# Attention: two-step value blocks, four maxima banks, and a denominator summed by GpSimd, DMA and one direct tile

## The reference, cut to what matters

```python
q, k, v = jnp.moveaxis(qkv, 2, 0)
scale = HD ** (-0.5)
attn = jnp.einsum('blhd,bmhd->bhlm', q, k) * scale
attn = jax.nn.softmax(attn, axis=-1)
out = jnp.einsum('bhlm,bmhd->blhd', attn, v).reshape(B, L, D)
```

## Time and profile before

| | before |
|---|---|
| median of 3 runs | 3703.89 us |
| lowest, highest | 3703.32, 3704.92 us |
| profiled execution, span | 3696.8 us |
| TensorE, weight loads, VectorE, ScalarE, GpSimd busy | 3452.4, 2197.3, 2266.1, 1552.4, 1775.8 us |
| attention's value blocks, first to last start | 994.5 to 2784.6 us |

### The profile page before, as it was taken

How to read it: one execution, slowest core, us unless ns; L and a number is a source line. 1 busy time by engine, 2 the same in 40 slices (tenths; PEclk the granted TensorE clock), 3 DMA queues, 4 the chain that set the end, 5 groups by cost and what they waited for, 6 DMA issues and landing times. The chain is left out here.

```text
span 3696.8 us, 51173 instructions
## 1 busy us (share of the span) xinstructions
PE 3452.4 (93%) x17516; PEld 2197.3 (59%) x17516; DVE 2266.1 (61%) x3547; ACT 1552.4 (42%) x2751; POOL 1775.8 (48%) x527
## 2 busy tenths in 40 slices
PE   7899996997999999999999999999995779999999
PEld 6488885775544444444444444444434658888887
DVE  1378874444978788788788887887715932222222
ACT  0111114341166666666656666666662242222222
POOL 1033321001288788787887887877885500000000
PEclk9999998997699999999999999999997889999999
DMA  4122224446201222102222022200004641111100
GB/s 163 66 93 88 91 80 172 172 158 183 46 17 34 43 47 44 38 16 44 47 48 44 7 44 47 47 10 13 7 6 154 216 146 68 40 40 40 37 32 23
DMA packets 158137, 250.59 MB, mean 68 GB/s; under 512 B 46939, under 2 KB 68699, under 8 KB 151774
## 3 DMA queue, kind: packets, MB, share of 16 engines
q1 hardware_dynamic: 147166, 230.96, 21.1%
q10 hardware_dynamic: 10752, 16.79, 1.5%
HBM read 158.89 MB, written 88.08 MB: 67 GB/s over the span
## 5 line engine op out<-in xcount | busy, mean ns | idle before, releaser
L1147 DVE TENSOR_REDUCE att_mx<-att_pM 128x1 f32<-128x512 f32 x2048 | 1267.9, 680 | 336.2 <-PE att_pM L1213 334.0
L1104 ACT ACTIVATE att_prob<-att_pS 128x512 f32<-128x512 f32 x2048 | 1080.4, 601 | 772.8 <-PE att_pS L1261 765.2
L1083 POOL TENSOR_TENSOR att_acc<-att_acc,att_prob 128x2048 f32<-128x2048 f32 x288 | 1327.5, 4609 | 129.2 <-ACT att_prob L1104 104.1
L1213 PE MATMUL att_pM<-att_ks,att_qs 96*128 96x512 f32 x2048 | 855.1, 432 | 54.7 <-DVE att_mx L1147 33.6
L1261 PE MATMUL att_pS<-att_qs,att_ks 98*128 98x512 f32 x2048 | 868.8, 430 | 10.2 <-ACT att_prob L1104 8.0
L1261 PEld LDWEIGHTS att_pS<-att_qs,att_ks 98*128 98x128 f32 x2048 | 386.2, 190 | 555.1 <-ACT att_prob L1104 385.7
L1228 PE MATMUL att_pO<-att_prob,att_V 128*32 128x512 f32 x4096 | 548.7, 608 | 0.7 <-ACT att_prob L1104 0.7
L1213 PEld LDWEIGHTS att_pM<-att_ks,att_qs 96*128 96x128 f32 x2048 | 405.4, 198 | 200.5 <-DVE att_mx L1147 120.3
L1627 DVE TENSOR_TENSOR mlp_us<-mlp_tu,mlp_us 128x512 fp32r<-128x512 f32 x128 | 89.7, 700 | 536.0 <-ACT mlp_us L1600 536.0
L1670 PE MATMUL mlp_pu<-mlp_hs,mlp_W 128*128 128x512 f32 x1536 | 370.7, 391 | 18.9 <-DVE mlp_W L1619 18.9
L1689 PE MATMUL mlp_pa<-mlp_W,mlp_us 128*128 128x512 f32 x1536 | 368.8, 389 | 0.0
(11 more groups left out here) (181 smaller groups left out, 2984.7 us busy)
## 6 DMA issues: line engine op xcount, KB each, us to landing
qk_d<-qkv_qs SPq DMA_DIRECT2D x64, 512.0 KB, 2.7
att_qs<-qk_d SPq DMA_DIRECT2D x48, 512.0 KB, 7.4
att_ks<-qk_d SPq DMA_DIRECT2D x48, 512.0 KB, 13.8
gat_xT<-in_xT SPq DMA_DIRECT2D x32, 256.0 KB, 3.1
gat_xrow<-in_x SPq DMA_DIRECT2D x32, 256.0 KB, 2.8
x_d<-gat_x SPq DMA_DIRECT2D x32, 256.0 KB, 2.1
qkv_xr<-x_d SPq DMA_DIRECT2D x8, 1024.0 KB, 5.8
v_d<-qkv_vs SPq DMA_DIRECT2D x32, 256.0 KB, 2.0
```

The costliest lines, as they stand in the source:

```text
L1083: nc.gpsimd.tensor_tensor(acc[half][:], old[:], new[:], ALU.add).then_inc(added, 1)
L1104: nc.scalar.activation(prob[step % PR][:, c, :], pS[n % 3][:], ACT.Exp, scale=SCALE).then_inc(exp_done, 1)
L1147: nc.vector.tensor_reduce(mx[:, n // 4, n % 4:n % 4 + 1], bank(g, n)[:], AX.X, ALU.max).then_inc(m_read, 1)
L1213: nc.tensor.matmul(bank(g, n)[:], qs[k][0:KD, h, t * P:(t + 1) * P], ks[k][0:KD, h, mc * 512:(mc + 1) * 512], start=True, stop=True).then_ ...
```

## The change

- **Values** are made for two steps at a time: at even steps, after the third score, TensorE runs the value blocks of the two steps before.
- **Maxima banks**: `pM` has four banks, filled in one sequence (`place`); `pZ` is gone.
- **Denominator**: of the 16 tiles of a half, nine are added by GpSimd in eight additions (tiles 0, 1, 3, 5, 7, 9, 11, 13, 14). Six (`SENT`: 2, 4, 6, 8, 10, 12) are gathered in a tile `gathered` by DMA: SP copies the first, GpSimd issues the other five as accumulating DMAs, each behind the landing of the one before. Tile 15 goes directly. At step 4 of the next half TensorE multiplies these three by ones in a score bank, which takes a turn between the scores (`turns_of`).
- **Reciprocal**: ScalarE copies the sums; SP copies one of each 32 equal rows, as 128x16, into `packed`; VectorE inverts that; SP writes it to DRAM (`z_d`) and spreads it back over `rec`. GpSimd makes the product with `oc`, between its additions.
- `prob` has eight buffers, `qs` and `ks` three. Stores of the result move from ScalarE's queue to SP's. The groups are written out, without the loop.

The diff, cut to its core:

```diff
-        U = 4
-        PR = 4
-        ADDED = [0, 1, 2, 4, 5, 6, 8, 9, 11, 12, 13]
-        FINISH = 2
-        INVERT = 4
+        U = 3
+        PR = 8
+        SENT = [2, 4, 6, 8, 10, 12]
+        LAST = MT - 1
+        ADDED = [t for t in range(LAST) if t not in SENT]
+        FINISH = 4
+        INVERT = 6
+        SCALED = 5
-        pM = [m.ps(f"pM{i}") for i in range(3)]
-        pO, pZ = m.ps("pO"), m.ps("pZ")
+        pM = [m.ps(f"pM{i}") for i in range(4)]
+        pO = m.ps("pO")
...
+            def send_first(n):
+                step = n % 2 * MT + SENT[0]
+                sp.wait_ge(exp_done, exps(n // 2, step))
+                if n >= 1:
+                    sp.wait_ge(exp_done, turns_of[n - 1] + 1)
+                sp.dma_start(gathered[:], prob[step % PR][:]).then_inc(first_sent, 16)
+            def reciprocals(n):
+                sp.wait_ge(exp_done, turns_of[n] + 1)
+                for c in range(4):
+                    row = rec[c * HD:c * HD + 1, :].rearrange("a (i x) -> a i x", x=16)
+                    sp.dma_start(packed[c * HD:(c + 1) * HD, :], row).then_inc(z_packed, 16)
+                sp.wait_ge(inverted, n + 1)
+                sp.dma_start(io["z_d"][n % 2].rearrange("c (i x) -> (c i) x", x=16), packed[:]).then_inc(z_kept, 16)
+                sp.wait_ge(z_kept, 16 * (n + 1))
+                for c in range(4):
+                    sp.dma_start(rec[c * HD:(c + 1) * HD, :], io["z_d"][n % 2, c:c + 1, :].to_broadcast([HD, 512])).then_inc(z_spread, 16)
...
+            def send(n, j):
+                step = n % 2 * MT + SENT[j]
+                pool.wait_ge(exp_done, exps(n // 2, step))
+                if j == 1:
+                    pool.wait_ge(first_sent, (n + 1) * 16)
+                else:
+                    pool.wait_ge(sent, (n * (len(SENT) - 1) + j - 1) * 16)
+                nc.gpsimd.dma_start(gathered[:], prob[step % PR][:], accum_op=ALU.add).then_inc(sent, 16)
...
+                        if ADDED[i] - 1 in SENT[1:]:
+                            send(n, SENT.index(ADDED[i] - 1))
+                        if i == SCALED and n >= 1:
+                            pool.wait_ge(added, n * NA + i)
+                            scale(n - 1)
...
+                elif t == SENT[0]:
+                    act.wait_ge(first_sent, (at // MT + 1) * 16)
+                elif t in SENT:
+                    act.wait_ge(sent, (at // MT * (len(SENT) - 1) + SENT.index(t)) * 16)
...
+            def invert(n):
+                dve.wait_ge(z_packed, 64 * (n + 1))
+                nc.vector.reciprocal(packed[:], packed[:]).then_inc(inverted, 1)
...
+                        if c == 2 and step % 2 == 0 and (g or step):
+                            behind(*divmod(g * ST + step - 2, ST))
+                            behind(*divmod(g * ST + step - 1, ST))
+                            if step % MT == FINISH and (g or step >= MT):
+                                finish(2 * g + step // MT - 1)
```

More of the change, by code:

```diff
@@ L1269, in body @@
+            for q in range(NM):
+                maxima(0, q)
+            for q in range(EARLY):
+                maxima(1, q)
+            top_of(0)
+            for q in range(EARLY, LEAD * 4):
+                maxima(1, q)
+            pe.wait_ge(cleared, 1 + U)
+            for g in range(NG):
+                pe.wait_ge(top_rows[g % U], (g // U + 1) * 32)
+                pe.wait_ge(v_loaded[g % 2], (g // 2 + 1) * 16)
                 for step in range(ST):
-                    if step == ST - LEAD + 1 and before(g, NG - 1):
+                    if step == ST - LEAD + 1 and g + 1 < NG:
@@ L1291, in _ @@
-            groups(pe, body)
-            behind(NG - 1, U - 1, ST - 1)
-            finish(NG, 0)
+                    for c in range(4):
+                        scores(g, step, c)
+                        if c == 2 and step % 2 == 0 and (g or step):
[3 more added lines that the diff above has]
+                                finish(2 * g + step // MT - 1)
```

402 lines of the change are left out of this document (202 added, 200 removed).

## The result

The change makes the kernel slower: 3755.61 us (median, 3751.48 to 3758.88) beside 3703.61 us for the kernel before on the same chip, a ratio of 1.0148 with a 95% interval of 1.0132 to 1.0163. The forecast was 3565 us.

The account below looks back on a forecast made before the run. TensorE was taken to bound 15 groups: 112.9 - 5.0 - 5.7 - 3.7 + 0.8 = 99.3, plus 4.5 = 103.8 us, x15 = -136.5; with the end, 3703.9 - 138.5 = 3565 us. Range 3505 to 3840, the forecast's own 3500 to 3625.

Parts of the forecast that it names:

- TensorE's sum: Attention groups: TensorE's time falls from 112.9 to 99.3 us a group, before any wait for packed sums.
- the fourth bank: Maxima in two-step blocks: four banks hold TensorE's lead of up to 1.5 us over VectorE, costed at nothing.
- The terms for the ones blocks and for VectorE: Per group: fewer ones blocks, all behind value blocks, save 5.7 us; TensorE's time lost to VectorE goes, 3.7 us.
- D: Gather chain: time from one accumulating send's issue to the next, taken as 6.6 us; up to 7.7 free.
- the formula: Gather chain: beyond D of 7.7 us, a half lasts 11.2 + 5D.
- Up to 4 us later, still in time: Fifth send sharing DMA engines with the load batch: up to 4 us later, within its 5 us margin.
- The late packed sums: Half with the loads: VectorE waits for sums packed behind the batch, +4.5 us once a group.
- The end: Last group and closing: last group saves 10 us; chain landing and three more copies for reciprocals cost 8.
- The signs: Right: groups 99 to 104 us, sends within 6.5; wrong: sends 8 apart, DMA-released exponentials, lower TensorE clock.
- Rival 1: Gather chain becomes the bound: D 8.9 us, group 121.3, time 3850 us; turns at D 8.05; chance 0.26.
- Rival 2: Chain fits outside the load batch, not in it: sends 4 us late, group 108, about 3630 us; chance 0.20.
- Rival 3: VectorE becomes the bound in eight-tile stretches: one more 2.5 us wait per half, 3640 us; chance 0.06.

Follow-up runs that it names:

- kernel 6: Changed kernel without the five accumulating sends (kernel 2), and with three maxima banks instead of four: 3583.56 us, ratio 0.969 to the kernel before.
- kernel 1: Changed kernel without the q, k and v loads of the later groups, stale data used again: 3598.64 us, ratio 0.9719 to the kernel before.
- kernel 9: Changed kernel with the five accumulating sends of each half issued as plain copies: 3514.82 us, ratio 0.9503 to the kernel before.
- kernel 2: Changed kernel without the five accumulating sends and the waits for them: 3503.46 us, ratio 0.9462 to the kernel before.
- kernel 4: Changed kernel with five gathered tiles (2, 4, 6, 8, 10) instead of six: 3691.65 us, ratio 0.9974 to the kernel before.
- kernel 11: Changed kernel with five gathered tiles spread out (2, 4, 7, 9, 12), loads as they were: 3630.52 us, ratio 0.9805 to the kernel before.
- kernel 8: Changed kernel, six gathered tiles, loads split and moved behind the last send of each half: 3629.04 us, ratio 0.9809 to the kernel before.
- kernel 10: Changed kernel with five gathered tiles spread out (2, 4, 7, 9, 12) and loads split behind last sends: 3546.95 us, ratio 0.9589 to the kernel before.
- kernel 12: Changed kernel, six gathered tiles, whole load batch waiting for the last send of the half before: 3728.47 us, ratio 1.0064 to the kernel before.
- kernel 3: Changed kernel with the group's loads issued later, behind the store of a result: 3735.96 us, ratio 1.009 to the kernel before.

## Why the prediction was wrong, point by point

**TensorE's sum was right.** With the sends away a group takes 99.8 us, forecast 99.3. The two-step blocks save the 5.0 us that I gave them (5.1), and the fourth bank covers what I said it does, at 5.0 us a group (kernel 6). The terms for the ones blocks and for VectorE (-5.7, -3.7) were tested only in the sum. Net of the waits that they bring, two-step blocks are worth only 3.1.

**The step that failed is the price D of one send and what the batch does to it.** I took D = 6.6 us on the assumption that half of the second read overlaps the first. It is 7.9 without loads in the half shown of kernel 1 and 8.1 in the mean of all its halves: 7.3 of landing, the rest issue and waiting. Kernel 9 shows the term that was too small: the addition costs 2.6 us, as much as a whole pass, and not 1.35. My sum called anything up to 7.7 free and thus gave this chain no cost; with D = 8.1 the half must be 51.8 and not 49.65 by the formula. Measured it is 52.2, which is the 4.6 us a group of kernel 1 against kernel 2. The Trainium skill (Collectives: The Full Stack, "The bandwidth ceiling: the fold count and why AG != RS != AR") says of the adding transfers of a collective that they read two sources and so run at half the rate. The time of a local addition in this trace agrees: less the 2.1 us of the earlier trace rows it is 5.2 us beside 2.6, and the D of 7.9 that I worked out from it and then did not take is nearly the measured one. For the plain copy the Trainium skill (DMA: Bandwidth & Descriptors, "Anatomy of one DMA - SWDGE (gpsimd) path") gives 2.0 us and bytes over 436 GB/s, an estimate of 4.4 us. The trace agrees: 4.4 at the least and 4.7 in the median (kernel 9).

**"Up to 4 us later, still in time"** was the second half of the same failure. I priced the send in the batch as sharing bandwidth fairly. It landed after 15.8 us in the stretch shown, after 18 us in kernel 4, up to 18.3 in kernel 11, about as long as the 17.5 us of the batch itself, though the send moves 1 MB beside its 3.5. That is +8 us and more for that send instead of 4, and the slack of 5 us was gone with D already. D also set how they meet: I had the fifth send go out 1 us ahead of the loads, and in the stretch shown it went out 7.7 us behind the first of them (1561.40 and 1569.15). It cost 10.3 us a group.

**The late packed sums** (+4.5) did not come: VectorE waited 0.8 us in 8.7 groups. In the changed kernel the sends were late first: the closing sum itself stood 7 us back, and by then the batch had passed (its last load landed at 1588.3, the packing was issued at 1591.77). But the term was too large as well. In kernels 2 and 9 no send is late and the loads stand where they stood, and yet VectorE waits for the packed sums only 15.6 and 16.6 us in ten groups. The line of kernel 2:

```profile
DVE att_packed L1236 <- DMA att_packed<-att_rec: 15.6, 11, 1.8
```

Their groups of 99.8 and 99.7 leave 0.5 us above the 99.3 for it, where I had 4.5. The mechanism as such exists: where the loads were moved behind a last send the waits are 56.2, 30.9 and 106.2 us in 1000 (kernels 8, 10 and 12).

**Together:** 99.8 + 4.6 + 10.3 = 114.7 where I had 99.3 + 0 + 4.5 = 103.8. The difference of 10.9, x15 = 163 us, is most of the 190.6 by which the forecast missed.

**The end** was the other miss: -2 forecast, +20.6 measured. From the last closing block on it is 2833.09 to 2852.01, 18.9 us, before 2789.92 to 2800.90, 11.0. These +7.9 look like my +8, but by luck: my 8 was to hold the landing of the chain as well. TensorE's timeline shows that landing, which comes on top:

```profile
2818.33 1.04 PE L1293 MATMUL att_pS<-att_prob,att_ones 128*32 128x512 f32 x8
2833.09 1.94 PE L1293 MATMUL att_pS<-att_gathered,att_ones 128*32 128x512 f32 x8 [13.72 <-DMA att_gathered<-att_prob]
```

TensorE is through with its scores and waits 13.72 us for the last of the sends, where it waited 3.89 us for GpSimd before: +9.8. With no more tiles to compute, nothing hides the chain's end. The remaining +2.9 stand ahead of these waits, where I had -10. I had taken the two halves of the last group to be bound by the chain at 44 us each. From one half's first send to the next's (2742.45 to 2794.82) it is 52.4, and in this stretch the chain is not what holds it: ScalarE's longest wait for a gather is 0.68 us (in the half before, 4.31).

```profile
2781.12 1.57 ACT L1204 ACTIVATE att_prob<-att_pS 128x512 f32<-128x512 f32 x3 [0.68 <-DMA att_gathered<-att_prob]
```

TensorE's value blocks follow each other after 5.43 us at full clock (2737.93 to 2743.36), so that eight of them and the closing blocks (2.6 us) ask for 46 us, more than my 44. From 2742 to 2764 the granted clock was 0.77 in the mean, and there they follow after some 7 us:

```profile
2743.36 3.54 PE L1287 MATMUL att_pO<-att_prob,att_V 128*32 128x512 f32 x16
...
2750.46 3.54 PE L1287 MATMUL att_pO<-att_prob,att_V 128*32 128x512 f32 x16
```

**The signs.** Of those named for wrong, all three were there: sends 8 us or more apart, exponentials released by a DMA, the clock at its lower level behind them. Of those for right only the block prices came.

**The rivals.** Rival 1 was the right mechanism: the chain of sends became the bound. It put its turning point at D = 8.05 with 9.9 us for the loads; measured were 8.1 (kernel 1, all halves) and 10.3, so the kernel sat just beyond it, at +52 us instead of the +146 of its D = 8.9. I gave it 0.26. Rival 2 had the collision in its place, but priced at 4 us. Rival 3 did not come: VectorE's own work holds TensorE up markedly only with three banks. What could have warned me stood in the text: two of its values of D (7.5 and 7.9) lay 0.2 us on either side of the 7.7 at which the cover ended, and I took one well inside.

What stays open: of the 10.3 us for the loads, only an estimate separates the waits from the lower clock behind them. From 1300 to 2300 TensorE is busy 880.4 us in the changed kernel at a granted clock of 0.94, and 950.6 in kernel 1 at 0.99. That is 101.0 of 114.7 us a group and 99.2 of 104.4, so some 1.7 us are instructions that take longer and some 8.5 are added idle time. No run here holds the clock up through such a wait. Nor did I try the six tiles spread further apart, or gathers that do not stand in series.

## What to carry to other kernels

Where work is moved to a chain of DMAs in series, price the chain by landing and not by bandwidth: count an accumulating copy as two passes unless a trace shows less (here 7.3 us beside 4.7), take the deadline of every buffer in it and not of the last alone, and treat a cover of a few tenths of a microsecond as none. Then look at what else the DMA engines do at that moment: a transfer that goes out into a large batch can land as late as the batch (here 1 MB in 3.5 MB, after 13 to 18 us). Here, leaving one tile to GpSimd, spreading the other sends to the pace of the chain and splitting the loads so that neither part meets a send turned a loss of 1.5% into a gain of 4.1%.

## What the runs showed of the hardware that I had not expected

- The same 1 MB from one SBUF tile to another, issued by GpSimd, lands after 4.7 us as a copy and after 7.3 us as an accumulation.
- A send of 1 MB in a load batch of 3.5 MB lands after 13 to 18 us (the changed kernel and kernels 3, 4 and 11). In kernel 12 even the issue of a copy behind the seven loads kept SP's queue for 12.59 us.
